# Gated cross-attention and mixture-of-experts block: the unrolled loop over 39 expert tiles becomes a counted loop on each engine

## Reference

```python
logits = flat @ router_w.T
weights = jax.nn.softmax(logits, axis=-1)
top_w, top_idx = jax.lax.top_k(weights, TOPK)                 # TOPK = 2 of E = 8
comb = zeros_like(weights).at[arange(N)[:, None], top_idx].add(top_w)
ge = einsum('nh,eih->nei', xb, wg); ue = einsum('nh,eih->nei', xb, wu)   # H = 512, I = 352, bf16
he = sigmoid(ge) * ue
de = einsum('nei,ehi->neh', he, wd)
routed = (comb[:, :, None] * de).sum(axis=1)
return x + shared_out + routed
```

## Time and profile before

| | us |
|---|---|
| median of 3 runs | 318.51 |
| lowest, highest | 317.33, 319.25 |
| the profiled execution | 318.51 |
| its span, first to last instruction | 316.8 |
| expert loop within it, about | 200.7 to 292.4 |

### The profile page before, as it was taken

How to read it: one execution, slowest core, us unless ns; L and a number is a source line. 1 busy time by engine, 2 the same in 40 slices (tenths; PEclk the granted TensorE clock), 3 DMA queues, 4 the chain that set the end, 5 groups by cost and what they waited for, 6 DMA issues and landing times.

```text
span 316.8 us, 5646 instructions
## 1 busy us (share of the span) xinstructions
PE 293.5 (93%) x1593; PEld 208.0 (66%) x1607; DVE 214.0 (68%) x580; ACT 131.9 (42%) x236; POOL 140.2 (44%) x163
## 2 busy tenths in 40 slices
PE   8598959999999999999999999899999999999990
PEld 3246737787787767877888788566666666665730
DVE  0757788658775538876886588467776767676094
ACT  3237257930656843463724651243434343433000
POOL 3702988175740185086078355024434343434200
PEclk9959999999999999999999999999999999999997
DMA  7999399611224011000992992334343434339598
GB/s 232 364 231 262 102 188 188 254 70 67 66 104 164 0 69 67 0 0 7 193 233 71 176 228 97 89 85 127 103 134 103 130 108 122 114 89 305 168 370 332
DMA packets 30492, 46.01 MB, mean 145 GB/s; under 512 B 2880, under 2 KB 20032, under 8 KB 30464
## 3 DMA queue, kind: packets, MB, share of 16 engines
q1 hardware_dynamic: 19888, 27.66, 28.5%
q0 software_dynamic: 10432, 17.99, 24.5%
q10 hardware_dynamic: 144, 0.00, 0.0%
HBM read 39.58 MB, written 14.72 MB: 171 GB/s over the span
## 4 chain that ended last, share of the span: by engine, by line
PE 71%; issue 9%; DVE 8%; POOL 6%; ACT 2%; DMA 2%; DVEq 0%; SPq 0%; POOLq 0%; ACTq 0%
PE bank L750 15%; PE bank L493 11%; PE bank L494 11%; PE bank L495 11%; PE bank L767 8%; POOL xg L428 5%; PE bank L505 4%; PE bank L488 4%; PE bank L740 3%; PE bank L758 2%; PE bank L628 1%; DVE prob L1076 1%; DVE acc L1434 1%; DMA xg<-lnb,slot 1%; POOL hT_lo L417 1%
## 5 line engine op out<-in xcount | busy, mean ns | idle before, releaser
L477 POOL DMA_INDIRECT z<-ysb,dest x39 | 37.2, 955 | 62.4 <-DVE ysb L1410 62.1
L1018 ACT ACTIVATE sigc<-bank 128x352 f32<-128x352 f32 x39 | 18.1, 463 | 54.2 <-PE bank L750 54.2
L1405 DVE TENSOR_TENSOR hrow<-sigc,bank 128x352 bf16<-128x352 f32 x39 | 20.3, 521 | 23.9 <-ACT sigc L1018 23.9
L428 POOL DMA_INDIRECT xg<-lnb,slot x32 | 31.7, 991 | 9.9 <-issue 7.3
L750 PE MATMUL bank<-wgu_lo,xTb 128*128 x156 | 36.0, 313 | 0.0
L750 PE MATMUL bank<-wgu_hi,xTb 128*128 x156 | 36.0, 312 | 0.0
L493 PE MATMUL bank<-lnT_hi,sgu_lo 128*128 128x512 f32 (+2 forms) x72 | 29.6, 411 | 1.6 <-DVE lnT_lo L1113 1.6
L767 PE MATMUL bank<-wd_sb,hTb 128*128 (+1 forms) x104 | 29.0, 381 | 1.1 <-issue 0.4
L1410 DVE TENSOR_SCALAR ysb<-bank,wt 128x512 bf16<-128x512 f32 x39 | 29.1, 747 | 1.0 <-PE bank L767 0.9
L495 PE MATMUL bank<-lnT_hi,sgu_hi 128*128 128x512 f32 (+2 forms) x72 | 28.4, 395 | 0.0
L494 PE MATMUL bank<-lnT_lo,sgu_hi 128*128 128x512 f32 (+2 forms) x72 | 28.3, 394 | 0.0
(11 more groups left out here) (186 smaller groups left out, 658.2 us busy)
## 6 DMA issues: line engine op xcount, KB each, us to landing
xt<-xg SPq DMA_DIRECT2D x39, 129.0 KB
xT_raw<-xT SPq DMA_DIRECT2D x4, 1024.0 KB, 7.3
acc<-x SPq DMA_DIRECT2D x4, 1024.0 KB, 9.5
out<-acc SPq DMA_DIRECT2D x16, 256.0 KB, 3.9
wgu_lo<-wguT POOLq DMA_DIRECT2D x2, 1408.0 KB, 13.3
wgu_hi<-wguT POOLq DMA_DIRECT2D x2, 1408.0 KB, 14.0
cx<-ctxT SPq DMA_DIRECT2D x4, 512.0 KB, 4.6
wd_sb<-wdT POOLq DMA_DIRECT2D x2, 1024.0 KB, 10.8
```

The costliest lines, as they stand in the source:

```text
L428: nc.gpsimd.indirect_dma_start(out=xg, out_offset=bass.IndirectOffsetOnAxis(ap=slot[:, c, j:j + 1], axis=0), in_=lnb[c][:, j, :], in_offse ...
L477: nc.gpsimd.indirect_dma_start(out=z, out_offset=bass.IndirectOffsetOnAxis(ap=dest[:, u:u + 1], axis=0), in_=ysb[:, r, :], in_offset=None) ...
L1018: act.activation(sigc[:, v, :], bank[2 * v][:, 0:I], ACT.Sigmoid).then_inc(s["csig"], 1)
L1405: V.tensor_tensor(hrow[:, v, 0:I], sigc[:, v, :], bank[2 * v + 1][:, 0:I], ALU.mult).then_inc(s["ch"], 1)
```

## The change

On every engine the middle of the expert loop becomes a counted loop (`Fori`), whose body is four tiles, and whose counter q is a register. `QN` = 9. SP, ACT and POOL run q = 1 to 8 in the loop (32 tiles, 7 jumps back), PE and DVE q = 2 to 8 (28 steps, 6 jumps back); the first tiles and the last stay written out. So in the loop

- each wait is against a register computed from q (`at_least`, `result`, `send`), and columns of `erow`, `epack_i`, `dest`, `again` and `wt` are addressed by a register;
- PE loads the experts at the start of an iteration, ahead of the step with r = 0, and uses them at once;
- POOL first copies the tile's column of `dest` to a fixed place, `desti`, waits for its own copy, and does one more small operation (`carrier`) before the indirect DMA, whose indices are now `desti`. It also waits for the DMA of the same slot four tiles before.

```diff
-            for u in range(SLOTS, NE):
+            with sp.Fori(1, QN) as q:
+                for r in range(SLOTS):
+                    load_tile(SLOTS * q + r, r, SLOTS * q + r - SLOTS + 1)
+            for u in range(SLOTS * QN, NE):
                 load_tile(u, u % SLOTS, u - SLOTS + 1)
...
-            def send(u, r):
+            def send(u, r, q):
                 pool.wait_ge(s["yev"], u + 1)
+                if q is not None:
+                    pool.wait_ge(s_yd[r], 16 * q)
...
+                nc.gpsimd.tensor_copy(desti[:, r:r + 1], dest[:, bass.ds(u, 1)]).then_inc(s["didx"], 1)
+                pool.wait_ge(s["didx"], u + 1)
+
+                nc.gpsimd.tensor_tensor(carrier[:], half[:], half[:], ALU.add)
                 nc.gpsimd.indirect_dma_start(
-                    out=z, out_offset=bass.IndirectOffsetOnAxis(ap=dest[:, u:u + 1], axis=0),
+                    out=z, out_offset=bass.IndirectOffsetOnAxis(ap=desti[:, r:r + 1], axis=0),
...
-            ids = experts(0)
-            for u in range(NE + 3):
-                q, r = divmod(u, SLOTS)
-                if r == SLOTS - 1 and u + 1 < NE + 3:
-                    coming = experts(q + 1)
-                step(q, r, ids)
-                if r == SLOTS - 1:
-                    ids = coming
+            for q in range(2):
+                ids = experts(q)
+                for r in range(SLOTS):
+                    step(q, r, ids)
+            with pe.Fori(2, QN) as q:
+                ids = experts(q)
+                for r in range(SLOTS):
+                    step(q, r, ids)
+            for u in range(SLOTS * QN, NE + 3):
+                if u % SLOTS == 0:
+                    ids = experts(u // SLOTS)
+                step(u // SLOTS, u % SLOTS, ids)
...
-            for u in range(NE + 2):
+            for r in range(SLOTS):
+                step(0, r)
+            with act.Fori(1, QN) as q:
+                for r in range(SLOTS):
+                    step(q, r)
+            for u in range(SLOTS * QN, NE + 2):
                 step(u // SLOTS, u % SLOTS)
...
-                V.tensor_tensor(dest[:, u:u + 1], xt[:, r, DST:DST + 1], again[:, u:u + 1], ALU.max)
+                V.tensor_tensor(dest[:, bass.ds(u, 1)], xt[:, r, DST:DST + 1], again[:, bass.ds(u, 1)], ALU.max)
...
-            for u in range(1, NE + 3):
+            for u in range(1, 2 * SLOTS):
+                step(u // SLOTS, u % SLOTS)
+            with dve.Fori(2, QN) as q:
+                for r in range(SLOTS):
+                    step(q, r)
+            for u in range(SLOTS * QN, NE + 3):
                 step(u // SLOTS, u % SLOTS)
```

More of the change, by code:

```diff
@@ L37, in at_least @@
 def at_least(eng, sem, n):
-    if n > 0:
+    if not isinstance(n, int) or n > 0:
         eng.wait_ge(sem, n)
@@ L291, in load_tile @@
                     sp.wait_ge(s["xev"], free)
[L292 removed]
+                row = sp.value_load(erow[0:1, bass.ds(u, 1)], min_val=0, max_val=E * REG)
                 sp.dma_start(xt[:, slot_, :], xg[bass.ds(row, P), :]).then_inc(s_xl[slot_], 16)
@@ L473, in _ @@
             scatter(last_b, 1)
-            def send(u, r):
+            def send(u, r, q):
                 pool.wait_ge(s["yev"], u + 1)
+                if q is not None:
+                    pool.wait_ge(s_yd[r], 16 * q)
+                if isinstance(u, int) and u >= SLOTS * QN:
+                    nc.gpsimd.indirect_dma_start(
+                        out=z, out_offset=bass.IndirectOffsetOnAxis(ap=dest[:, u:u + 1], axis=0),
+                        in_=ysb[:, r, :], in_offset=None).then_inc(s_yd[r], 16)
+                    return
+                nc.gpsimd.tensor_copy(desti[:, r:r + 1], dest[:, bass.ds(u, 1)]).then_inc(s["didx"], 1)
+                pool.wait_ge(s["didx"], u + 1)
+                nc.gpsimd.tensor_tensor(carrier[:], half[:], half[:], ALU.add)
                 nc.gpsimd.indirect_dma_start(
-                    out=z, out_offset=bass.IndirectOffsetOnAxis(ap=dest[:, u:u + 1], axis=0),
+                    out=z, out_offset=bass.IndirectOffsetOnAxis(ap=desti[:, r:r + 1], axis=0),
                     in_=ysb[:, r, :], in_offset=None).then_inc(s_yd[r], 16)
-            for u in range(NE):
-                send(u, u % SLOTS)
+            for r in range(SLOTS):
+                send(r, r, None)
+            with pool.Fori(1, QN) as q:
+                for r in range(SLOTS):
+                    send(SLOTS * q + r, r, q)
+            for u in range(SLOTS * QN, NE):
+                send(u, u % SLOTS, QN)
         @block.tensor
@@ L743, in wide @@
             def wide(u, v, e):
-                if u == 1:
+                if isinstance(u, int) and u == 1:
                     pe.wait_ge(s["hid"], IT * NB)
@@ L761, in narrow @@
             def narrow(u, v, e):
-                if u == 0:
+                if isinstance(u, int) and u == 0:
                     pe.wait_ge(s["shared"], LT * last_b)
@@ L772, in step @@
                 u = SLOTS * q + r
-                if 2 <= u <= NE + 1:
+                known = isinstance(u, int)
+                if not known or 2 <= u <= NE + 1:
                     turn_hidden(u - 2, r % 2)
-                if u >= 3:
+                if not known or u >= 3:
                     narrow(u - 3, (r - 3) % 2, ids[r])
-                if u + 1 < NE:
+                if not known or u + 1 < NE:
                     rows_in(u + 1, (r + 1) % SLOTS, q + 1 if r == SLOTS - 1 else q)
-                if u < NE:
+                if not known or u < NE:
                     wide(u, r % 2, ids[r + SLOTS - 1])
@@ L1026, in step @@
                 u = SLOTS * q + r
-                if 1 <= u <= NE:
+                known = isinstance(u, int)
+                if not known or 1 <= u <= NE:
                     sigmoid(u - 1, (r - 1) % 2)
-                if 2 <= u <= NE + 1:
+                if not known or 2 <= u <= NE + 1:
                     hidden_out(u - 2, r % 2)
-            for u in range(NE + 2):
+            for r in range(SLOTS):
+                step(0, r)
+            with act.Fori(1, QN) as q:
+                for r in range(SLOTS):
+                    step(q, r)
+            for u in range(SLOTS * QN, NE + 2):
                 step(u // SLOTS, u % SLOTS)
@@ L1408, in result @@
                 dve.wait_ge(s["cy"], u + 1)
-                at_least(dve, s_yd[slot_], 16 * q)
-                V.tensor_scalar(ysb[:, slot_, :], bank[6 + v][:, :], wt[:, u:u + 1].bitcast(F32), None,
+                if not isinstance(q, int) or q > 0:
+                    dve.wait_ge(s_yd[slot_], 16 * q)
+                V.tensor_scalar(ysb[:, slot_, :], bank[6 + v][:, :], wt[:, bass.ds(u, 1)].bitcast(F32), None,
                                 ALU.mult).then_inc(s["yev"], 1)
@@ L1414, in step @@
                 u = SLOTS * q + r
-                if 1 <= u <= NE:
+                known = isinstance(u, int)
+                if not known or 1 <= u <= NE:
                     hidden(u - 1, (r - 1) % 2)
-                if 3 <= u:
+                if not known or 3 <= u:
                     result(u - 3, (r - 3) % 2, (r - 3) % SLOTS, q if r == 3 else q - 1)
-                if u + 1 < NE:
+                if not known or u + 1 < NE:
                     rows_out(u + 1, (r + 1) % SLOTS)
```

9 lines of the change are left out of this document (6 added, 3 removed).

## The result

| | before | changed |
|---|---|---|
| median of 22 runs each, us | 318.30 | 319.47 |
| lowest, highest | 315.01, 319.88 | 317.50, 322.13 |
| ratio, 95% interval | | 1.0053 (1.0029 to 1.0078) |
| span of the profiled execution | 316.8 | 318.6 |

The changed kernel is slower by 0.5%, 0.9 to 2.5 us. I had forecast 4.0 us (322.5), in a range from 319 to 346: the right sign and the right place, and more than twice the size.

What follows compares the result with a forecast made beforehand. PE was taken to bound the expert loop, its sequencer having no lead left at the experts load. 318.5 + 3.2 (iteration edges) + 0.8 (register waits) = 322.5 us; own range 320.2 to 326, 8-in-10 range 319 to 346.

Steps and rivals of the forecast that it cites:

- the right sign: Whole kernel: the changed one is slower, 322.5 us against 318.5, 1.3%; chance of slower 0.86.
- the right place: PE's iteration edge, beside the experts load: bookkeeping costs 0.46 us at each of 6 jumps back, 3.2 with entering and leaving.
- a reserve of fixed size: PE's sequencer: a lead of about 0.6 us over the array; the load eats it all, more beside it adds time.

Runs made afterwards that it cites:

- e6: Changed kernel with a second, unused load of the experts at the start of each of PE's iterations; ratio 1.0223 to the kernel before.
- e12: Changed kernel with PE's loop placed so its 213 instructions lie in one packet, not two; ratio 1.0088 to the kernel before.
- e3: Changed kernel with DVE's copy to xTb ahead of its scaling to ysb; ratio 1.0006 to the kernel before.
- e2: Changed kernel with PE unrolled as in the kernel before, all other engines looped; ratio 0.9969 to the kernel before.
- e4: Kernel before, unrolled, with DVE's copy to xTb ahead of its scaling; ratio 0.9964 to the kernel before.
- e11: Kernel before, unrolled, with DVE's copy to xTb first and each experts load ahead of r = 0, not r = 3; ratio 0.9973 to the kernel before.
- e13: Kernel before with two more waits, on semaphores reached long before, in the middle of each PE wide; ratio 1.0057 to the kernel before.
- e9: Changed kernel with a second, unused load of the experts in the middle of PE's body, behind r = 1; ratio 1.0219 to the kernel before.

## What to carry to other kernels

A sequencer's lead isn't a reserve of fixed size: it grows by array time less sequencer time in each tile, it stops at the wait that ends last, and each register instruction behind that wait comes off it. This is read from one kernel and its variants. Before costing control flow at a loop's edge, find that wait, and add up the sequencer's instructions over the whole iteration, gaps included (an instruction of 32 or 51 ns takes 0.09 to 0.13 us). And keep a register load and a jump apart, or release earlier what the sequencer waits for; here the order of two DVE operations was worth 1.4 us with the loop and 1.5 without, where the loop's loss was 2.0.

## What the chip showed besides

- A compare-and-branch on PE takes 0.218 us when taken, in one packet or across two, and 0.079 when not. On DVE, POOL, ACT and SP it takes 0.056, 0.053, 0.045 and 0.045 us in the median.
- The first jump back was mostly longer than the others (2.95 for 2.76 in the changed kernel, 3.9 for 3.5 in e6, 2.83 for 2.76 in e12). In the first two the load there is longer too (0.38 for 0.30 to 0.31, 0.58 for 0.30), in e3 (2.90 for 2.57) it is not; it is not explained.
- A load into a register took 0.30 to 0.62 us. In the profiled execution of the kernel before it was 0.36 in the median, in those of e2, e4, e11 and e13, unrolled on PE too, 0.30, in e9 at the edge 0.61. So the 0.36 may be that execution's and not the kernel's. What holds a load was not found; it is by itself worth 0.1 to 0.3 us at a place with no lead.
